# The causal mask moves from TensorE products into the vector engine's row maximum, and the order of the score units alternates between pairs

## The reference, cut to what matters

```
Q, K = apply_rope(Q), apply_rope(K)
scores = einsum('bhqd,bhkd->bhqk', Q, K) / sqrt(d_k)
scores = where(causal, scores, -inf)          # key later than query: masked
attn = softmax(scores, axis=-1)
out = einsum('bhqk,bhkd->bhqd', attn, V)
```

## Time and profile before

| | |
|---|---|
| median of 3 runs | 1963.16 us (1962.06 to 1966.38) |
| the profiled execution | 1963.09 us, its span 1961.4 us |
| TensorE products, busy share of the span | 84% |
| vector engine | 52% |
| ScalarE | 36% |
| POOL | 29% |
| mean granted TensorE clock, share of full speed | 0.923 |

### The profile page before, as it was taken

One profiled execution on the slowest core, in us unless ns is written; L12 is line 12 of the kernel. 1 busy time (PEld: TensorE's weight loads), 2 busy tenths in 40 slices (PEclk: granted clock), 3 DMA queues, 4 the chain that ended last, 5 costly groups with the idle time before them and its releaser, 6 DMA issues. The chain is left out here.

```text
span 1961.4 us, 29495 instructions
## 1 busy us (share of the span) xinstructions
PE 1638.4 (84%) x9849; PEld 1093.9 (56%) x9849; DVE 1024.0 (52%) x2339; ACT 699.0 (36%) x1457; POOL 565.0 (29%) x995
## 2 busy tenths in 40 slices
PE   1999999947999996884799999999999479959910
PEld 0577777644666664442455555555555268848810
DVE  1344445451222223885776666666664258855533
ACT  0444444311222221221065566565556211134400
POOL 2223433350000004883122322222322125510056
PEclk9899999978999997986899999999999789979965
DMA  8001111022222214676645655655552475445444
GB/s 304 20 22 33 49 49 54 33 88 68 64 65 65 65 52 144 217 253 206 94 55 77 103 73 72 96 82 75 94 71 39 130 206 158 146 148 159 151 130 149
DMA packets 151056, 204.05 MB, mean 104 GB/s; under 512 B 20608, under 2 KB 119424, under 8 KB 150656
## 3 DMA queue, kind: packets, MB, share of 16 engines
q1 hardware_dynamic: 104304, 131.12, 30.3%
q10 hardware_dynamic: 34320, 37.50, 5.6%
q0 software_dynamic: 12288, 33.57, 5.4%
HBM read 116.91 MB, written 84.93 MB: 103 GB/s over the span
## 5 line engine op out<-in xcount | busy, mean ns | idle before, releaser
L1690 DVE TENSOR_REDUCE t_row_max<-t_ps_s 128x1 f32<-128x1024 f32 (+7 forms) x512 | 382.0, 757 | 179.8 <-PE t_ps_s L1737 171.9
L1706 ACT ACTIVATE t_probs<-t_ps_st 128x512 f32<-128x512 f32 x576 | 325.6, 596 | 228.9 <-PE t_ps_st L1751 227.2
L1751 PE MATMUL t_ps_st<-t_qs,t_ks 128*128 128x512 f32 (+3 forms) x768 | 277.2, 408 | 0.8 <-ACT t_probs L1706 0.5
L1669 POOL TENSOR_SCALAR_AFFINE_SELECT t_probs<-t_probs 128x128 f32<-128x128 f32 x512 | 139.1, 299 | 395.0 <-ACT t_probs L1706 392.3
L1735 PE MATMUL t_ps_s<-t_ks,t_qs 96*128 96x512 f32 (+3 forms) x768 | 233.5, 358 | 2.2 <-DVE t_row_max L1690 1.9
L1751 PEld LDWEIGHTS t_ps_st<-t_qs,t_ks 128*128 128x128 f32 x768 | 132.0, 192 | 126.5 <-ACT t_probs L1706 100.4
L1767 PE MATMUL t_ps_o<-t_probs,t_vs 128*17 128x256 f32 (+1 forms) x2560 | 185.0, 363 | 0.4 <-issue 0.4
L1349 POOL DMA_INDIRECT d_ye<-outputs_dram,r_pos_all x64 | 64.7, 1011 | 326.1 <-POOLq L1112 308.2
L1735 PEld LDWEIGHTS t_ps_s<-t_ks,t_qs 96*128 96x128 f32 x768 | 136.2, 190 | 21.8 <-DVE t_row_max L1690 15.0
L849 PE MATMUL ps_h<-w_in,xnt 128*128 128x512 f32 x256 | 126.0, 617 | 23.5 <-ACT xnt L683 23.5
L1144 PE MATMUL m_ps_h<-w_sb,m_xt 128*128 x284 | 135.4, 600 | 0.0
(11 more groups left out here) (315 smaller groups left out, 2752.8 us busy)
## 6 DMA issues: line engine op xcount, KB each, us to landing
m_x_t<-gathered_dram SPq DMA_DIRECT2D x150, 128.0 KB, 2.0
outputs_dram<-m_y ACTq DMA_DIRECT2D x150, 128.0 KB, 1.7
t_qs<-qkt_dram SPq DMA_DIRECT2D x128, 128.0 KB, 5.9
t_ks<-qkt_dram SPq DMA_DIRECT2D x128, 128.0 KB, 6.6
qkt_dram<-d_hi SPq DMA_DIRECT2D x32, 256.0 KB, 4.1
qkt_dram<-d_lo SPq DMA_DIRECT2D x32, 256.0 KB, 4.1
headst_dram<-t_att SPq DMA_DIRECT2D x32, 256.0 KB, 7.6
x_t<-in_x_dram SPq DMA_DIRECT2D x8, 512.0 KB, 4.6
```

What stands on the lines that cost most here:

```text
L1669: nc.gpsimd.affine_select(out=diag, in_=diag, compare_op=ALU.is_ge, fill=0.0, base=0, pattern=[[1, P]], channel_multiplier=-1).then_inc(ma ...
L1690: nc.vector.reduce_max(row_max[:, p % 2, head * NC + qc:head * NC + qc + 1], ps_s[i % 2][:, 0:(qc + 1) * P], AXX).then_inc(unit_ready, 1)
L1706: nc.scalar.activation(probs[:, p % 2, i // NST, base:base + STC], ps_st[i % 2][:], ACT.Exp, scale=HD ** -0.5).then_inc(exp_ready, 1)
L1751: last = nc.tensor.matmul(ps_st[i % 2][:, col:col + width], ks[:, at, kc * P:(kc + 1) * P], qs[:, at, q0:q0 + width], start=True, stop=True)
```

## The change

The row maximum becomes one operation of two steps, `tensor_tensor_reduce`: it adds a table in SBUF to the scores in PSUM, and takes the maximum of the sums. The table `later` is now f32 and 1024 columns wide: zero, but for the last 128 columns, which hold the old tile. A unit of width w takes its last w columns. The sums are also written out, as bf16, to a new buffer `seen`, which nobody reads. The mask product and the identity `ident_b` go, with their fill and select. TensorE waits only for the fills; the vector engine waits for the select.

The list of units becomes two lists. Even pairs have the old order; in odd pairs head 0 goes from narrow to wide and head 1 from wide to narrow, so that widths are 128, 1024, 256, 896 and so on to 1024, 128. The slots of chunks, averages and units are the same.

```diff
-    later = sb("t_later", [P, P], BF16)
-    ident_b = sb("t_ident_b", [P, P], BF16)
+    later = sb("t_later", [P, NC * P])
+    seen = sb("t_seen", [P, 2, NC * P], BF16)
...
-    units = [u for i in range(NC) for u in ((0, NC - 1 - i), (1, i))]
+    units = [[u for i in range(NC) for u in ((0, NC - 1 - i), (1, i))], [u for i in range(NC) for u in ((0, i), (1, NC - 1 - i))]]
...
             nc.gpsimd.memset(later[:], 0.0).then_inc(filled, 1)
-            nc.gpsimd.memset(ident_b[:], 0.0).then_inc(filled, 1)
             nc.gpsimd.memset(vs[:], 1.0).then_inc(filled, 1)
-            pool.wait_ge(filled, 6)
-            nc.gpsimd.affine_select(out=later[:], in_=later[:], compare_op=ALU.is_ge, fill=-1.0e30, base=0,
-                                    pattern=[[-1, P]], channel_multiplier=1).then_inc(set_up, 1)
-            nc.gpsimd.affine_select(out=ident_b[:], in_=ident_b[:], compare_op=ALU.not_equal, fill=1.0, base=0,
+            pool.wait_ge(filled, 5)
+            last_keys = later[:, (NC - 1) * P:]
+            nc.gpsimd.affine_select(out=last_keys, in_=last_keys, compare_op=ALU.is_ge, fill=-1.0e30, base=0,
                                     pattern=[[-1, P]], channel_multiplier=1).then_inc(set_up, 1)
...
-            dve.wait_ge(filled, 6)
+            dve.wait_ge(set_up, 1)
...
-                for i, (head, qc) in enumerate(units):
+                for i, (head, qc) in enumerate(units[p % 2]):
                     dve.wait_ge(s_done, NU * p + i + 1)
-                    nc.vector.reduce_max(row_max[:, p % 2, head * NC + qc:head * NC + qc + 1],
-                                         ps_s[i % 2][:, 0:(qc + 1) * P], AXX).then_inc(unit_ready, 1)
+                    width = (qc + 1) * P
+                    at = head * NC + qc
+                    nc.vector.tensor_tensor_reduce(out=seen[:, i % 2, 0:width], in0=ps_s[i % 2][:, 0:width],
+                                                   in1=later[:, NC * P - width:], scale=1.0, scalar=-3.0e38, op0=ALU.add,
+                                                   op1=ALU.max, accum_out=row_max[:, p % 2, at:at + 1]).then_inc(unit_ready, 1)
...
                     last = nc.tensor.matmul(ps_s[i % 2][:, k0:k1], qs[0:MAX_ROW, at, qc * P:(qc + 1) * P], ks[0:MAX_ROW, at, k0:k1],
-                                            start=True, stop=k1 < width)
-                last = nc.tensor.matmul(ps_s[i % 2][:, qc * P:width], ident_b[:], later[:], start=False, stop=True)
+                                            start=True, stop=True)
...
-            pe.wait_ge(filled, 6)
+            pe.wait_ge(filled, 5)
             pe.wait_ge(q_zeroed, 1)
-            pe.wait_ge(set_up, 2)
```

More of the change, by code:

```diff
@@ L1585, in attention @@
     NR = len(lanes[0])
-    NU = len(units)
+    NU = len(units[0])
     NX = 2 * NST
@@ L1620, in row @@
                 if p == 0:
-                    sp.wait_ge(filled, 6)
+                    sp.wait_ge(filled, 5)
                     sp.wait_ge(q_zeroed, 1)
@@ L1726, in unit @@
             def unit(p, i):
-                head, qc = units[i]
+                head, qc = units[p % 2][i]
                 at = 2 * (p % RINGQ) + head
```

## The result

The changed kernel took 1929.1 us (median of four runs, 1925.9 to 1932.4) against 1962.6 (four runs, 1961.3 to 1966.4); the ratio is 0.9826 with a 95% interval of 0.9801 to 0.9851. Forecast were 1928 and a range of 1914 to 1944. The profiled execution took 1926.69 us, its span is 1924.9.

A forecast was written before the change was run, and what follows sets the result against it. TensorE was taken to bound the attention stage, each step ending by its own work or the maximum's chain. Full ticks 33.1, ticks 0 to 2 1.2 and set-up 0.7 us sum to 35.0: 1963.1 - 35.0 = 1928, range 1914 to 1944.

The forecast's parts named there:

- The mask products: On TensorE, 16 products a tick (one pair of heads) removed, 0.07 to 0.13 us each: 1.49 us a tick.
- own work: TensorE's own time per tick, without the 0.26 us wait and the mask products: 17.74 - 0.26 - 1.49 = 15.99 us.
- The maximum: Vector engine's new row maximum: old rate of 1.04 ns a column, fixed cost +0.06 us, bounds +0 and +0.16.
- the +0.16 end: Upper bound of the maximum's fixed cost, as if a separate small operation of 0.157 us followed each; time 1941 us.
- The chain steps: Unit, its maximum, next unit on the same PSUM buffer; waits of 0.71 us in even ticks, 0.51 in odd.
- Ticks 0 to 2: First three ticks, without averaging and nearer to the chain: 0.4 us gain each, 1.2 in all, bounds 0 to 1.5 each.
- Set-up: Before the first units, TensorE waits only for the fills, until 944.21 and not 945.04: 0.7 us earlier.
- (a): Rival: maximum's fixed cost +0.16 us, ticks near 17.2 and 16.9, 1941 us; lower end +0, 1922; within the forecast's 0.82.
- (b): Rival: the maximum doesn't end the steps, TensorE's own work alone counts; 53 us less, 1910 us; chance 0.04.
- (c): Rival: on the vector engine the new maximum needs twice the time a column; 21.6 us a tick, about 2090; chance 0.06.
- (d): Rival: the alternating order does nothing, all ticks 16.70 us, 1931 us; inside the range, within the forecast's 0.82.
- (e): Rival: waits of 0.1 to 0.4 us lower TensorE's clock; given no chance of its own.

The follow-up runs named there:

- the 128-column kernel: Changed kernel with a plain maximum over only the last 128 columns of each unit, against the kernel before: 1909.8 us, ratio 0.9714.
- the three others of this order and maximum: Changed kernel with POOL's weight masks ahead of the value copy (1928.3 us), with the averages spread (1930.1 us), and run again unaltered (1933.2 us).

## Why the prediction was right

**The mask products: right per product, wrong in one subtraction.** With the products back the kernel is as slow as before, so they are the gain. The 0.07 and 0.13 us show as forecast: averages 0.07 ahead of the unit's end, chunk ends 0.24 after the narrow unit (0.23 forecast; behind a unit of 128 columns 0.29, which is the 0.07 to 0.08 taken there). But own work is 16.14 a tick, not 15.99. The missing 0.15 is one step: unit 0 to 2 takes 1.83 of own work by the 128-column kernel, where I had 2.09 - 0.26 - 0.155 = 1.68. I had taken the listed 0.26 wait of the weight load out whole; only some 0.10 of it (2.09 - 1.83 - 0.155) lengthened the step, since TensorE's products were still running while the load waited. The other steps of even ticks were right (2 to 4: 1.85 forecast, 1.84 measured); in odd ones the step from 1 to 3 takes 1.92 where I had 1.83.

**The maximum: mechanism right, size too high in all steps but one.** No slope was added, and of the fixed cost that I took at 0.06 (the bounds were 0 and 0.16) 0.01 is there in every step. Only the step from unit 0 of an even tick has 0.05, and 0.04 of it stands ahead of the pass. The operations of the earlier trace rows with a third operand pay their 0.05 in the pass itself; this one's second record lies over the pass's end. The Trainium skill ("VectorE: DVE Perf Modes", Two Vector instructions with no wait between them) says that it is two instructions; the trace agrees, with 453 reads of 83 ns. What I made of it, the +0.16 end, doesn't follow: two instructions without a wait between them aren't two durations in a row.

**The chain steps** were forecast for even ticks as 2.08, 1.99, 1.71 and 1.89 (units 0 to 2, 2 to 4, 11 to 13, 13 to 15) and came out as 2.06, 1.87, 1.69 and 1.76. The two of 896 columns are 0.12 to 0.13 shorter. 0.06 of it I had too much in the maximum; the other 0.07 is the 0.11 from a unit's end to its maximum. I had read it at unit 0 and used it everywhere, and it is 0.04 at units 2, 11 and 13. First before (mask end 1119.34, maximum at 1119.38), then changed (unit end 1106.11 + 0.67 = 1106.78, maximum at 1106.83):

```profile
1119.11 0.23 PE L1737 MATMUL t_ps_s<-t_later,t_ident_b 128*128 128x128 bf16 x1
1119.38 1.09 DVE L1690 TENSOR_REDUCE t_row_max<-t_ps_s 128x1 f32<-128x896 f32 x1 [0.64 <-PE t_ps_s L1737]
```
```profile
1106.83 1.09 DVE L1690 CUSTOM_DVE_ANT_0 t_seen<-t_ps_s,t_later 128x896 bf16<-128x896 f32 x1 [0.55 <-PE t_ps_s L1736]
```

The last 0.06, from the maximum to the next unit, holds in each of these steps but that from 11 to 13, where nothing waits. In odd ticks the 1024-wide unit isn't unit 0, so its step came out at 1.96 against 2.08.

**The sum.** Even ticks 16.59 (16.70 forecast), odd 16.43 (16.50): the own work too low by 0.15, the waits too high by 0.26 (0.45 against 0.71) and 0.22 (0.29 against 0.51). These two aren't independent. In the step from unit 0 to 2 the chain is the longer of the two clocks, so that the 0.15 missing in the own work could only appear as 0.15 too much wait; the step itself was 0.02 off. What is left is the 0.11 by which the chain was too long in an even tick, 0.07 in an odd one. Full ticks gave 29 x 1.23 = 35.7, less 2.0 for the two long ticks, 33.7, against 33.1. Ticks 0 to 2 gave 0.6 instead of 1.2: 14.83, 14.82 and 16.38, before 16.49, 14.62 and 15.55. Tick 0 gained 1.7, where I had 0.4. A part of this is the clock, which rose earlier behind the set-up: in the second 4 us from the first unit, before and changed,

```profile
949.70:953.70 4.00, 4.00 (x19) 2.69 (x18) 2.66 (x4) 0.00 (x0) 2.25 (x7) 0.78 1.04 121
```
```profile
946.47:950.47 4.00, 3.78 (x18) 2.69 (x17) 3.46 (x9) 0.00 (x0) 2.81 (x8) 1.00 1.04 115
```

Tick 2 lost 0.8 in this profile, in which the clock fell, and 0.1 or less in the three others of this order and maximum. Set-up gave 0.8 (941.81 against 945.04, less the 2.46), against 0.7. Together 35.1 against 35.0. That they agree this well is partly luck: the full ticks gave 2.6 more than forecast, and the long ticks, which no step of mine had, took 2.0 and ticks 0 to 2 another 0.6.

**The rivals.** (a) fell with the accumulator's read: its ticks of 17.2 and 16.9 are excluded. Its lower end, ticks of 16.40, is nearer, but plain maxima don't reach it in even ticks either. (b) fell: the chain costs 0.37 a tick, and the kernel without it comes to 1909.8, where (b) stood at 1910. (c) fell: no halving, 1225 ns for 1024 columns. (d) gives the right time for another reason: the order does shorten odd ticks, and gives half of it back in tick 1. (e), to which I gave no chance of its own: the clock did fall in tick 2, before the full ticks, for about 0.7 us more in this profile than in the three others; I had looked at the clock where TensorE is full, not where it has gaps. That the waits caused it isn't shown. The chances of (a) to (d) as listed come to 0.90 for faster and 0.06 for slower, not 0.89 and 0.07. What no step of mine had was POOL's queue: I compared POOL's busy share, 131 of 500, and not how long its one waiting instruction holds 17 others.

## What to carry to other kernels

Price small products by where their neighbours end, not by their own record: 0.23 us in the record, 0.07 to 0.13 in the time. A listed wait isn't what the step loses: a step's own work is measured by making the chain short (here a maximum over 128 columns), and that one kernel gave both the error of my sum and the 20 us that were left. Where a buffer of several banks is freed as a whole, let the reader and the next writer go bank by bank before anything is moved about in the order.

## What the runs showed of the hardware

- A pass of the vector engine that adds an f32 operand from SBUF to one in PSUM, writes bf16 and keeps the maximum takes what a plain reduction takes: 1225 ns for 1024 columns (plain 1225) and 289 for 128 (plain 286). Its accumulator's read is a record of 83 ns, of which 0.01 us shows behind the pass.
- From the end of a unit's last product to the start of its maximum it is 0.04 us where the vector engine is idle (units 2, 11 and 13 of even ticks, 1 and 3 of odd ones), but 0.11 (plain maximum) or 0.15 (with the mask) for a tick's first unit, wide or narrow.
- The granted clock fell to 0.50 in tick 2 in all four profiles with the masked maximum, the alternating order and no filler; in the changed kernel's it fell behind and in stretches in which TensorE was busy 2.87 and 3.03 of 4 us (12 products each). It stayed at 1.00 with 2.98 of 4 in the old order, and with 2.65 and 2.90 (11 and 14 products) with the plain maximum. What decides is left open.
- Taking away a wait of TensorE in one place (averages spread, 0.38 us at unit 2 of even ticks) brought one of 0.32 at unit 15, with the tick unchanged to 0.01 us.
